# Merging two halves of a row maximum by a reduction instead of an elementwise maximum, and Newton steps with a per-partition scalar instead of a second tensor

## What is computed

```
x = x + deformable_conv(group_norm(x))            # 9 taps, bilinear samples at learned offsets
t = tokens(x)                                     # 8 images x 1024 tokens x 64 features
t = t + attention(layer_norm(t))                  # 16 heads of 64, rotary embedding, causal softmax
t = t + spectral(layer_norm(t))                   # 4 causal convolutions with 16 filters, plus 3 taps
```

```
q, k = rope(x @ wq), rope(x @ wk)
att  = softmax(where(causal, q @ k.T / 8, -inf))
y    = att @ v ;   out += y @ wo
```

## Time and profile before

| | |
|---|---|
| median of 3 runs | 3067.74 us (3067.49 to 3069.47) |
| the profiled execution: its time, its span | 3066.54 us, 3064.8 us |
| front stage and `AHEAD`, until the loop | about 248 us |
| the attention loop, 64 half-passes | about 248 to 2383 us |
| spectral stage | about 2425 to 3064 us |
| busy TensorE / VectorE / ScalarE / GpSimd, share of the span | 91% / 74% / 43% / 57% |
| the same in the loop (247 to 2383 us, 2136 us long) | 2030.9 / 1709.1 / 931.4 / 1488.2 us |
| granted TensorE clock: whole span, loop | 0.959, 0.99 |

### The profile page before, as it was taken

One profiled execution on the slowest core, in us unless ns is written; L12 is line 12 of the kernel. 1 busy time (PEld: TensorE's weight loads), 2 busy tenths in 40 slices (PEclk: granted clock), 3 DMA queues, 4 the chain that ended last, 5 costly groups with the idle time before them and its releaser, 6 DMA issues. The chain is left out here.

```text
span 3064.8 us, 60697 instructions
## 1 busy us (share of the span) xinstructions
PE 2777.3 (91%) x18761; PEld 1797.9 (59%) x18761; DVE 2275.0 (74%) x3909; ACT 1328.6 (43%) x1788; POOL 1735.3 (57%) x1832
## 2 busy tenths in 40 slices
PE   3548999999999999999999999999999699999998
PEld 1334555555555555555555555555555588888887
DVE  3547877878778878887878887787788576767676
ACT  1103444444444444444444444444444265656565
POOL 3745766766666677676767667766676581000000
PEclk8658999999999999999999999999999899999999
DMA  5531221222222222122222222224434543434343
GB/s 148 159 93 46 61 60 50 66 56 59 64 56 60 59 60 61 52 65 57 59 61 60 60 55 63 59 55 62 59 60 57 126 158 127 147 119 155 121 145 110
DMA packets 159644, 249.21 MB, mean 81 GB/s; under 512 B 71662, under 2 KB 93502, under 8 KB 159582
## 3 DMA queue, kind: packets, MB, share of 16 engines
q1 hardware_dynamic: 125902, 155.61, 17.8%
q0 software_dynamic: 33680, 92.71, 12.5%
HBM read 230.65 MB, written 17.04 MB: 81 GB/s over the span
## 5 line engine op out<-in xcount | busy, mean ns | idle before, releaser
L1085 ACT ACTIVATE attention_probs<-attention_pss 128x1024 f32<-128x1024 f32 x576 | 589.7, 1024 | 332.0 <-PE attention_pss L922 319.6
L1289 POOL DMA_INDIRECT attention_gat<-table,attention_idx x585 | 556.8, 952 | 200.2 <-issue 126.8
L922 PE MATMUL attention_pss<-attention_kq 64*128 64x512 f32 (+3 forms) x3072 | 652.1, 483 | 0.0
L1024 PE MATMUL attention_psY<-attention_probs,attention_xt 128*64 128x512 f32 (+3 forms) x3120 | 575.3, 497 | 0.2 <-issue 0.2
L1151 DVE TENSOR_REDUCE attention_mx<-attention_pss 128x2 f32<-128x1024 f32 (+3 forms) x520 | 513.6, 1020 | 45.4 <-PE attention_pss L922 45.4
L1246 POOL TENSOR_TENSOR attention_kq<-attention_tA,attention_tB 128x512 f32<-128x512 f32 x260 | 415.1, 1605 | 217.3 <-DVE attention_tB L1161 208.1
L1645 DVE SCALAR_TENSOR_TENSOR spectral_eo<-spectral_psE,kept_sig,spectral_eo 64x512 fp32r<-64x512 f32 x512 | 384.0, 750 | 170.1 <-ACT spectral_eo L1620 163.9
L1538 PE MATMUL spectral_psE<-spectral_tz,spectral_up 128*128 128x512 f32 (+1 forms) x2304 | 461.8, 358 | 6.6 <-DVE spectral_up L1636 6.4
L922 PE MATMUL attention_pss<-attention_rows_m,attention_ones 64*128 64x512 f32 (+2 forms) x1536 | 459.3, 530 | 0.0
L1620 ACT ACTIVATE spectral_eo<-spectral_psE,kept_sig 64x512 fp32r<-64x512 f32 x512 | 349.9, 683 | 244.6 <-PE spectral_psE L1538 239.7
L1538 PEld LDWEIGHTS spectral_psE<-spectral_tz,spectral_up 128*128 128x128 f32 x2304 | 386.2, 189 | 79.0 <-issue 7.2
(11 more groups left out here) (193 smaller groups left out, 3114.7 us busy)
## 6 DMA issues: line engine op xcount, KB each, us to landing
spectral_tz<-phis SPq DMA_DIRECT2D x128, 320.5 KB, 4.6
spectral_tz<-phis SPq DMA_DIRECT2D x128, 320.0 KB, 4.2
attention_xb<-xn SPq DMA_DIRECT2D x132, 256.0 KB, 3.8
attention_gat<-table,attention_idx POOLq DMA_INDIRECT x585
table<-front_pixT SPq DMA_DIRECT2D x32, 288.0 KB
attention_wt<-in_w SPq DMA_DIRECT2D x66, 128.0 KB, 3.6
attention_xt<-xt SPq DMA_DIRECT2D x18, 128.0 KB, 2.1
attention_xs<-in_x SPq DMA_DIRECT2D x65, 32.0 KB
```

The source lines that it names most:

```text
L922: ins = pe.matmul(out(n), left(rows), right(rows), **flags)
L1024: ins = pe.matmul(psY[C * n:C * n + C, q:q + w], xt[:, kt, :], probs[:, u, n, at:at + w], start=(u < 2), stop=(u == NU - 1), skip_group_ch ...
L1085: act.activation(probs[:, u[1], :, :].rearrange("p n q -> p (n q)"), pss[:, slot, :], ACT.Exp, scale=float(E) ** -0.5).then_inc(s_act, 1)
L1289: pool.indirect_dma_start(gat[:, n, :, :].rearrange("p q c -> p (q c)"), None, d.table.rearrange("r q c -> r (q c)"), bass.IndirectOffsetO ...
```

## The change

The far maxima of the query tiles 4 to 7 and their near ones are written side by side, into a new tile `mx_half` with a last axis of two, and `merge` is a `tensor_reduce` over that axis. The elementwise maximum with its two SBUF sources goes. In `norm`, the first and the third instruction of each Newton step take one of the two factors as a scalar per partition, in the form that the second one has. The number of instructions, their order, and all waits are the same.

```diff
-        mx_far = sb("mx_far", [P, 2, NT // 2])
+        mx_half = sb("mx_half", [P, 2, NT // 2, 2])
...
-                            ins = dve.tensor_reduce(mx_far[:, :, i - 4] if k0 else mx[:, :, i], scores, AX.X, ALU.max)
+                            ins = dve.tensor_reduce(mx[:, :, i] if i < 4 else mx_half[:, :, i - 4, k0 // 4], scores, AX.X, ALU.max)
...
                 def merge(seen):
 
                     dve.wait_ge(s_dve, seen)
-                    dve.tensor_tensor(mx[:, :, NT // 2:NT], mx[:, :, NT // 2:NT], mx_far[:, :, :], ALU.max).then_inc(s_mx, 1)
+                    dve.tensor_reduce(mx[:, :, NT // 2:NT], mx_half[:, :, :, :], AX.X, ALU.max).then_inc(s_mx, 1)
...
                     for _ in range(NEWTON):
-                        step(dve.scalar_tensor_tensor(out=fix[:, :], in0=rstd[:, :], scalar=-0.5, in1=rstd[:, :],
-                                                      op0=ALU.mult, op1=ALU.mult))
+                        step(dve.tensor_scalar(fix[:, :], rstd[:, :], rstd[:, 0:1], -0.5, ALU.mult, ALU.mult))
                         step(dve.tensor_scalar(fix[:, :], fix[:, :], var[:, 0:1], 1.5, ALU.mult, ALU.add))
-                        step(dve.tensor_tensor(rstd[:, :], rstd[:, :], fix[:, :], ALU.mult))
+                        step(dve.tensor_scalar(rstd[:, :], rstd[:, :], fix[:, 0:1], None, ALU.mult))
```

## The result

The changed kernel takes 2945.25 us (median, 2944.58 to 2945.84), where the kernel before takes 3068.37 us (3067.49 to 3069.47): the ratio is 0.9598, with a 95% interval of 0.9582 to 0.9615. The profiled execution has a span of 2944.1 us against 3064.8. The forecast was 2946 us.

A forecast was written before the change was run, and what follows sets the result against it. The prediction took TensorE's work plus its wait at row for merge to bound the loop. Savings of 94.5 us (earlier row) and 27.3 us (clock), 121.8 us, from the profiled 3066.5 us gave 2944.7, forecast 2946 us, range 2933 to 2985.

The forecast's parts named there:

- What bounds the loop: Attention loop: TensorE's own work plus its standstills, nearly all at row waiting for merge, 64 times, 89.4 us.
- Part 1, the merge: Merge on VectorE: as a one-source reduction not held by GpSimd, 0.170 instead of 1.541 us, ending 1.37 us earlier.
- The slope behind the forecast: Merge's reduction time: 1.07 ns a number, from reductions of 4 numbers (157 ns, SBUF) and 256 (427 ns, PSUM).
- Part 2, the Newton steps: Nine Newton instructions in norm: 214 ns each, the two holds gone, 0.105 us gained a half-pass and passed on to merge.
- How they reach TensorE: Row on TensorE: 1.48 us earlier per half-pass, 94.5 us in all; GpSimd's slack before its rope addition falls to about 0.5 us.
- Part 3, the clock: TensorE's clock: 16 falls behind row of k = 1, before the loop's branch, go with the wait, saving 27.3 us.
- The sum: Whole kernel: 94.5 us from the earlier row plus 27.3 us from the clock, 121.8 us saved.
- The rule on 2-port modes: Newton steps: rule that float32 tensor_scalar queues for GpSimd's port pair, set aside; by it 0.22 us lost, not 0.105 gained.
- the falls stay: Rival on TensorE's clock: the wait at row goes but the clock still falls, 2973 us; chance 0.10.
- another wait takes a part: Rival: slower reduction, held Newton forms or GpSimd's additions take back 16, 21 or up to 32 us; chance 0.11.
- the reduction is held too: Rival at merge: it still ends with GpSimd's addition, so no effect, 3068 us; chance 0.06.
- slower: Rival at merge: held reduction lets GpSimd's second addition in ahead, ending about 0.9 us later, 3125 us; chance 0.03.

The follow-up runs named there:

- The run with the merge alone: Changed kernel with its Newton steps put back as before the change, the merge still a reduction: 2951.65 us, ratio 0.9620 to the kernel before.
- The pair of k = 0 and k = 1: Changed kernel with the elementwise merge back in only one kind of half-pass: k = 0 alone 2992.57 us; k = 1 alone, where the loop's branch follows, 3013.69 us.
- the run with eight numbers: Changed kernel with rstd and fix eight numbers wide instead of one, first guess included: 3086.70 us, ratio 1.0057 to the kernel before.
- runs with eight numbers: Changed kernel with rstd and fix eight wide: first with the first guess eight wide too, 3086.70 us; then with that guess one number wide, 3030.05 us.
- the late copy of 63: Changed kernel with VectorE's copy of the normed tile moved from the end of norm to behind merge: 2971.50 us; written as a reduction, 2942.14 us, repeated 2939.92 us.

## Why the prediction was right

- **What bounds the loop.** That TensorE stood still 1.40 us a half-pass for a merge of eight numbers, and that nothing else replaced that wait, is borne out: no wait at L966 is left in the loop.
- **Part 1, the merge.** Forecast 170 ns, measured 170. The slope behind the forecast mixes a row out of SBUF with one out of PSUM, which no run supports; only 13 of the 170 ns hung on it, so that the fit to the nanosecond is in part luck. The cause was argued from the ends of instructions that coincide; the run with GpSimd's additions put first showed it, since the merge's length followed GpSimd's order. That a series without a gap counts as one hold is only half right: the last section has the numbers.
- **Part 2, the Newton steps.** Forecast 0.105 us a half-pass and 6.7 us in all, given the new merge. The run with the merge alone is 6.4 us slower than both together.
- **How they reach TensorE.** Forecast 1.48 us; the half-passes are 1.44 to 1.48 us shorter (32.61 to 31.15, 33.1 to 31.62, 33.48 to 32.04). GpSimd's slack in k = 0 was forecast at 0.5 us and is 0.54.
- **Part 3, the clock.** All 16 falls are gone. From the first to the last `row` of the loop it is 1980.0 us instead of 2099.3, 119.4 us less: 2072.0 - 1980.0 = 92 is the wait, and 27 the clock. The reason was less sure than the number: the forecast knew the falls by their company. The pair of k = 0 and k = 1 confirms that company, the run with eight numbers has falls without the branch, and why one standstill brings a fall and the next does not is open.
- **The sum.** Forecast 121.8 us; the two profiled spans differ by 120.7.
- **The rule on 2-port modes.** Here the reason was too broad, and the number came out by luck of the shape. I read from L1200 that an instruction with a single source is not held. With eight numbers per partition instead of one the same form is held, by additions, by selects and by indirect DMAs: the gain of 4% falls to 1.3% with the steps eight wide, and becomes a loss of 0.6% with the first guess eight wide as well. What protects the new forms is that they work on one number per partition. The kernel before had a row that said so of the very form that the steps now take (VectorE, inside the select of the earlier trace rows); it took 212 to 216 ns in all 192 places:

```profile
1509.96 0.21 DVE L1205 TENSOR_SCALAR attention_fix<-attention_fix,attention_var 128x1 f32<-128x1 f32 x1
```

- **The condition that was left out.** The Trainium skill (VectorE: DVE Perf Modes, "Mode 2×_2P — use both read ports for one tensor") puts `tensor_scalar` and `tensor_copy` from SBUF to SBUF into this mode, float32 included, if the outermost non-unit dimension is even, or odd and equal for source and destination. The runs with eight numbers and the late copy of 63 agree with it. One number per partition has no such dimension, and the prediction left this condition out when it said that by the rule the new forms would be held. That `tensor_reduce` runs in its plain mode alone (the Trainium skill, VectorE: DVE Perf Modes, "The perf-mode tier table (the rule you actually need)") agrees with the merge at 169 to 172 ns and the copy at 218 to 220 ns beside the same GpSimd work.

Of the rivals, "the falls stay" is refuted by the clock of 1.00 in the changed loop, "another wait takes a part" by the merge at 170 ns, the Newton forms at 214 ns and GpSimd's remaining 0.54 us, "the reduction is held too" and "slower" by the merge's row.

## What to carry to other kernels

Where a short VectorE instruction between SBUF tensors shows a microsecond, look at what GpSimd ends at the same moment. In these runs it is the form that decides: two SBUF tensors, or a copy or `tensor_scalar` of more than one number, wait for GpSimd, while a reduction or a one-column `tensor_scalar` does not; a reduction over an axis of one or two can do the work of a copy or a maximum. Before moving such an instruction, see what GpSimd does at the new place, and count a standstill of TensorE twice: for itself and for the clock that may fall behind it.

## What the runs showed of the hardware that was not expected

- An indirect DMA on GpSimd (0.95 us) holds a one-source VectorE instruction of more than one number until the DMA instruction ends, if the VectorE instruction starts late in it: 0.44 instead of 0.23 us at 0.50 us in (runs with eight numbers), and the copy of 63 numbers 0.52 to 0.54 instead of 0.19 us at 0.43 us in (first run with eight numbers). There is no hold at 0.23 us in, nor of that copy at 0.35 to 0.37 us in (the kernel before). So the limit lies between 0.37 and 0.43 us. The old Newton step with two SBUF tensors was not held by it: in the half-pass of the earlier trace rows the third L1203 began 0.53 us into such a DMA and took 0.16 us. Additions and selects hold both kinds.
- It matters which GpSimd instruction ends. Behind an addition the held instruction gets in, though the select that follows is recorded as beginning 0.04 us before the addition's end (L1203 in the earlier trace rows, in all 64 places). Behind a select that another select or an addition follows as closely it does not: the merge and the late copy are held over select, select and addition, 1.55 and 1.70 us, in all 64 places. Why is open.
- The same wait of 1.4 us costs 1.48 us a half-pass with the clock at 1.00 (47.3 us for 32), and 2.1 us on average where the loop's branch adds 0.4 us behind it (68.4 us for 32). TensorE's clock can fall without the branch as well, behind a standstill of 1.1 us and one of 0.35 us (5 places in the first run with eight numbers).
